# New instruction orders on four engines: an attention quad spread over two steps, beside the scans and in the last attention

## The reference

```
# state space layer, per sequence: 512 channels e, 16 states n
dA = exp(d_t[..., None] * A)
state = state * dA + (d_t * u_t)[..., None] * B_t[:, None, :]
y_t = einsum('ben,bn->be', state, C_t)
...
# causal attention, 16 heads of 32
scores = einsum('bqhd,bkhd->bhqk', q, k) * HEAD_DIM ** -0.5
attn = softmax(where(causal, scores, min))
ctx = einsum('bhqk,bkhd->bqhd', attn, v)
x = x + ctx @ wo
h = rms(x, w_ln2); logits = h @ w_router      # then 8 experts, top 2, and a shared one
```

## Time and profile before

| what | us |
|---|---|
| median of 3 runs | 1896.81 |
| lowest, highest | 1896.38, 1898.08 |
| the profiled run, its time | 1897.27 |
| the profiled run, its span | 1895.4 |
| VectorE busy | 1183.1 |
| TensorE busy | 1530.6 |
| scans of sequences 1, 2, 3: first to last start | 170 each (168 the third) |

### The profile page before, as it was taken

One profiled execution on the slowest core, in us unless ns is written; L12 is line 12 of the kernel. 1 busy time (PEld: TensorE's weight loads), 2 busy tenths in 40 slices (PEclk: granted clock), 3 DMA queues, 4 the chain that ended last, 5 costly groups with the idle time before them and its releaser, 6 DMA issues.

```text
span 1895.4 us, 26612 instructions
## 1 busy us (share of the span) xinstructions
PE 1530.6 (81%) x9104; PEld 1167.9 (62%) x9104; DVE 1183.1 (62%) x1731; ACT 888.1 (47%) x1974; POOL 810.3 (43%) x809
## 2 busy tenths in 40 slices
PE   5255877777967777957777799879999999999994
PEld 2134544555645555635556566668788899999973
DVE  4689658987568887489873444343332556565545
ACT  4443345664456664366652366212111566666510
POOL 0586135653145542266532321114431455555544
PEclk8555886888977888958887899989999999999997
DMA  5620000110100111001103200562220676777464
GB/s 192 244 75 26 23 6 25 60 51 28 46 17 34 51 46 31 27 23 51 45 29 117 89 29 29 195 233 83 99 85 1 223 270 234 269 236 267 151 232 160
DMA packets 94486, 195.74 MB, mean 103 GB/s; under 512 B 8769, under 2 KB 25665, under 8 KB 91025
## 3 DMA queue, kind: packets, MB, share of 16 engines
q1 hardware_dynamic: 89232, 177.26, 27.0%
q0 software_dynamic: 5120, 16.78, 2.6%
HBM read 140.40 MB, written 53.61 MB: 102 GB/s over the span
## 4 chain that ended last, share of the span: by engine, by line
PE 42%; issue 5%; DVE 5%; POOL 3%; ACT 2%; DMA 0%; DVEq 0%; ACTq 0%; SPq 0%; POOLq 0%
PE scores L588 20%; PE bank L588 12%; PE bank L770 2%; POOL yab L2162 2%; PE scores L707 2%; PE bank L720 1%; PE bank L652 1%; PE bank L735 1%; DVE YA L1552 1%; PE bank L960 1%; DVE HS L1542 1%; PE scores L710 1%; ACT PT L1180 1%; ACT bank L1137 1%; POOL lal L2155 1%
## 5 line engine op out<-in xcount | busy, mean ns | idle before, releaser
L1996 POOL TENSOR_TENSOR GB<-DU,BB 128x512 f32<-128x512 f32 x256 | 327.6, 1292 | 125.7 <-DVE HS L1542 67.6
L652 PE MATMUL bank<-ident,HS 128*128 128x128 f32 x896 | 184.9, 342 | 172.9 <-DVE YA L1552 118.0
L1542 DVE TENSOR_TENSOR_SCAN HS<-bank,GB 128x512 f32<-128x512 f32 x224 | 273.0, 1219 | 47.6 <-ACT bank L1137 23.9
L652 PEld LDWEIGHTS bank<-ident,HS 128*128 128x128 f32 x896 | 125.0, 172 | 222.3 <-DVE YA L1552 157.1
L1137 ACT ACTIVATE bank<-DL,aneg 128x512 f32<-128x512 f32 x224 | 154.9, 692 | 131.5 <-DVE HS L1542 130.2
L1552 DVE SCALAR_TENSOR_TENSOR YA<-bank,Ct,YA 128x512 f32<-128x512 f32 x224 | 164.3, 733 | 28.6 <-PE bank L652 26.5
L1180 ACT ACTIVATE PT<-bank 128x128 f32<-128x128 f32 (+3 forms) x256 | 110.5, 432 | 128.6 <-PE bank L720 125.9
L588 PE MATMUL scores<-xth,wgh 128*128 128x256 f32 x552 | 158.0, 286 | 2.0 <-DVE fa L1878 1.1
L588 PE MATMUL scores<-xth,wgl 128*128 128x256 f32 x552 | 156.1, 283 | 0.0
L588 PE MATMUL scores<-xtl,wgh 128*128 128x256 f32 x552 | 156.0, 283 | 0.0
L720 PE MATMUL bank<-ident,EX 128*128 128x128 f32 x640 | 129.8, 303 | 27.9 <-ACT PT L1180 25.8
(11 more groups left out here) (272 smaller groups left out, 3697.0 us busy)
## 6 DMA issues: line engine op xcount, KB each, us to landing
wgr<-wffn_in SPq DMA_DIRECT2D x108, 384.0 KB, 6.4
wdr<-wffn_in SPq DMA_DIRECT2D x81, 256.0 KB, 2.9
BB<-b_scratch SPq DMA_DIRECT2D x64, 256.0 KB, 3.2
xg<-V SPq DMA_DIRECT2D x1, 11776.0 KB, 40.2
xr<-xg SPq DMA_DIRECT2D x23, 512.0 KB, 5.7
yg<-ysb SPq DMA_DIRECT2D x23, 512.0 KB, 6.3
hah<-hhd SPq DMA_DIRECT2D x5, 1024.0 KB, 5.7
hal<-hhd SPq DMA_DIRECT2D x5, 1024.0 KB, 8.7
```

Source lines behind the costliest of these rows:

```text
L652: mm = nc.tensor.transpose(state_bank(s, q)[:, et * P:(et + 1) * P], HS[:, n % 2, et, tt * P:(tt + 1) * P], ident[:])
L1542: nc.vector.tensor_tensor_scan(HS[:, n % 2, et, :], decay_bank(s, k), GB[:, k % 4, :], 0.0, ALU.mult, ALU.add).then_inc(scan_done, 1)
L1996: nc.gpsimd.tensor_tensor(GB[:, k % 4, :], DU[:, et, :], BB[:, n % 2, :], ALU.mult).then_inc(gb_ready, 1)
```

## The change

The loop in `round_` is replaced on TensorE, ScalarE, VectorE and GpSimd by two functions on each, `units` (attention beside scans, three rounds) and `last_units` (attention 3). The round of scans alone keeps its order. The same instructions are issued with the same operands and waits, none is added or removed, and SyncE's order is as before. What differs is the order on each of the four engines. In `units`, k = 4q:

```diff
+            def units(b, s):
+                for q in range(-2, NQ + 1):
+                    now, next_, last = 0 <= q < NQ, 0 <= q + 1 < NQ, 0 < q
+                    i, m = quad(q)
+                    row = i - 1 if now and i else None
+                    if now:
+                        turn(b, HG * q + 1)
+                    if last:
+                        turn_states(s, T4 * (q - 1) + 1)
+                    if now:
+                        turn(b, HG * q + 2)
+                    if row is not None and m != 1:
+                        finish(b, row, (0, None, 1, 2)[m])
+                    if last:
+                        turn_states(s, T4 * (q - 1) + 2)
+                    if now:
+                        turn(b, HG * q + 3)
+                    if last:
+                        turn_states(s, T4 * (q - 1) + 3)
+                    if now:
+                        weigh(b, q)
+                    if next_:
+                        turn(b, HG * (q + 1))
+                    if now:
+                        turn_states(s, T4 * q)
+                    if q + 2 < NQ:
+                        scores(b, q + 2)
...
+            def last_units(b):
+                for q in range(-1, NQ):
+                    i, m = quad(q)
+                    if q + 1 < NQ:
+                        scores(b, q + 1)
+                    for a in range(HG):
+                        if q > 0:
+                            next(shared)
+                        if q >= 0 and a < HG - 1:
+                            turn(b, HG * q + a + 1)
+                        if q >= 0 and i and (m, a) in ((0, 1), (2, 1), (3, 2)):
+                            finish(b, i - 1, (0, 0, 1, 2)[m])
+                    if q + 1 < NQ:
+                        turn(b, HG * (q + 1))
+                    if q >= 0:
+                        weigh(b, q)
```

On ScalarE, `units`, and of `last_units` the part in which the tanh now stands ahead of the last `keep_turned`:

```diff
+            def units(b, s):
+                for q in range(-1, NQ + 1):
+                    now, next_ = 0 <= q < NQ, q + 1 < NQ
+                    i, m = quad(q)
+                    row = i - 1 if now and i else None
+                    v, w, k = HG * q, HG * (q + 1), T4 * q
+                    if now:
+                        keep_turned(b, v + 2)
+                    if next_:
+                        probs(b, w)
+                        probs(b, w + 1)
+                    if now:
+                        decay(s, k + 3)
+                        keep_turned(b, v + 3)
+                    if next_:
+                        probs(b, w + 2)
+                    if row is not None and m in (0, 2):
+                        finish(b, row, m + 1)
+                    if 0 < q + 1 < NQ:
+                        decay(s, k + 4)
+                    if next_:
+                        probs(b, w + 3)
+                    if now:
+                        keep_inverse(b, q)
+                    if next_:
+                        keep_turned(b, w)
+                        decay(s, k + 5)
+                    if row is not None and m == 1:
+                        finish(b, row, 2)
+                    if now:
+                        context(b, q)
+                    if next_:
+                        keep_turned(b, w + 1)
+                        decay(s, k + 6)
+                    if now and m == 3 and i + 1 < T4:
+                        finish(b, i, 0)
...
+                    if more:
+                        probs(b, w)
+                    keep_turned(b, v + 2)
+                    if more:
+                        probs(b, w + 1)
+                    for n in range(SE):
+                        if gate_end(n)[0] == q:
+                            early_tanh(n)
+                    keep_turned(b, v + 3)
+                    if more:
+                        probs(b, w + 2)
+                        probs(b, w + 3)
+                    if i and m == 2:
+                        finish(b, i - 1, 3)
+                    if m == 3 and more:
```

On VectorE, `units`; in `last_units`, `invert(q)` now stands at the start of quad q and the row's sum ahead of the shared expert's steps:

```diff
+            def units(b, s):
+                for q in range(-2, NQ + 1):
+                    now, next_, last = 0 <= q < NQ, 0 <= q + 1 < NQ, 0 < q
+                    i, m = quad(q)
+                    row = i - 1 if now and i else None
+                    k = T4 * q
+                    if row is not None and m == 3:
+                        finish(b, row, 3)
+                    if row is not None and m == 0:
+                        finish(b, row, 1)
+                    if last:
+                        add_state(s, k - 2)
+                    if row is not None and m == 2:
+                        finish(b, row, 2)
+                    if now:
+                        scan(s, k + 3)
+                    if last:
+                        add_state(s, k - 1)
+                    if next_:
+                        scan(s, k + 4)
+                    if now:
+                        context(b, q)
+                        add_state(s, k)
+                    if next_:
+                        invert(b, q + 1)
+                        scan(s, k + 5)
+                    if q + 2 < NQ:
+                        row_max(b, q + 2)
+                    if now:
+                        add_state(s, k + 1)
+                    if next_:
+                        scan(s, k + 6)
```

More of the change, by code:

```diff
@@ L869, in round_ @@
                     rotate(b, 7)
[L870 to L885 removed]
+                if att and scn:
+                    units(b, s)
+                elif scn:
+                    for q in range(NB):
+                        turn_states(s, q)
+                else:
+                    last_units(b)
                 if scn:
[L887 to L888 removed]
                     for tt in range(T4):
@@ L1337, in round_ @@
-                if att:
-                    keep_inverse(b, NQ - 1)
-                    context(b, NQ - 1)
-                if s == B:
-                    early_round(SE - 1)
+                if att and scn:
+                    units(b, s)
+                elif scn:
+                    for k in range(1, NB):
+                        decay(s, k)
+                        if k % 8 == 0 and k <= 8 * KC:
+                            round_weights(k // 8 - 1)
+                else:
+                    last_units(b)
@@ L1656, in early_ends, with last_units @@
                         early_up(n)
+            def units(b, s):
+                for q in range(-2, NQ + 1):
+                    now, next_, last = 0 <= q < NQ, 0 <= q + 1 < NQ, 0 < q
+                    i, m = quad(q)
+                    row = i - 1 if now and i else None
[26 more added lines that the diff above has]
+                        scan(s, k + 6)
+            def last_units(b):
+                row_max(b, 0)
+                for q in range(NQ):
+                    i, m = quad(q)
+                    more = q + 1 < NQ
+                    invert(b, q)
+                    if q:
+                        context(b, q - 1)
+                    if more:
+                        row_max(b, q + 1)
+                    if q == 0:
+                        low_down(0)
+                    if i and m == 0:
+                        finish(b, i - 1, 1)
+                    early_ends(q, False)
+                    if i and m > 1:
+                        finish(b, i - 1, m)
+                    early_ends(q, True)
+                context(b, NQ - 1)
             def round_(b, s):
```

214 lines of the change are left out of this document (78 added, 136 removed).

## The result

| | before | after |
|---|---|---|
| median, us | 1897.44 (1896.38 to 1898.5, 4 runs) | 1852.95 (1851.52 to 1853.62, 4 runs) |
| span of the profiled run | 1895.4 | 1851.2 |
| mean granted clock of TensorE | 0.861 | 0.878 |

The ratio of the times is 0.9761 [0.9747, 0.9775]: 44.5 us less, where 28.3 were forecast. The forecast of 1869.0 us was 16 us too slow.

The account below looks back on a forecast made before the run. VectorE's chain beside the scans was taken to bound the three rounds, TensorE attention 3. 1897.3 less 26.4 (three rounds of 13.9 - 5.1 = 8.8) less 1.9 gave 1869.0 us; forecast 1858 to 1882 (0.50), full range 1847 to 1894.

Parts of the forecast that it names:

- The stalls beside the scans: VectorE's waits for transposed states, scores, router product and first exponents beside the scans go: 13.9 us per round at full clock.
- What comes back at the lower clock: Row tiles 2 and 3, TensorE at 1.2 GHz 30% of the time: 5.1 us per round return, bounds 0 to 17.0.
- The floor doesn't move: VectorE's stall-free quad beside the scans stays at 9.28 us, since instructions and bank are the same; context only changes interval.
- rival 2: Waits move beside the scans: context late for its inverse, half a microsecond in 12 quads, 6 us a round; 1887 us, chance 0.18.
- The 1.6 us go: Start of a round: the first scan stands ahead of invert(0), so VectorE's 1.6 us wait for the first quad's exponents goes.
- Its scores are issued earlier: Beside the scans, scores two quads ahead come earlier while row_max comes behind the second next scan; 4.8 us of waits vanish.
- Rival 3: Slower: scores and a turn between two turn_states delay add_state beside the scans at the lower clock; 1909.6 us, chance 0.13.
- Net 1.9 us gained: Attention 3 as a whole: copies hidden in some quads, tanh in the way in others; bounds 8.1 gained and 3 lost.
- 6 x 0.5 = 3.0 us lost: Attention 3, six quads with a tanh: the last keep_turned queues behind it, making about 1.0 us where 0.54 stood.
- The 4.9 us saved: Attention 3, quads without tanh: the copy ahead of weigh is hidden, 9 x 0.54 us.
- Rival 1: Denser steps keep TensorE's upper clock, so all 41.7 us of stalls beside the scans go; 1847.5 us, chance 0.12.
- The signs: Expected in the changed profile: scan spans, the waits of nm, YA, invert and L731's instruction, and the first scan's start.

Follow-up runs that it names:

- experiment 7: Changed kernel with invert of the next quad ahead of the scan it now follows, as in the kernel before: 1855.97 us, ratio 0.9781.
- Experiments 2 to 4: Changed kernel with scores directly behind weigh again (1937.19 us), with row_max directly behind context again (1917.17 us), and with both (1903.87 us).
- experiment 2: Changed kernel with TensorE's scores of quad q + 2 directly behind weigh again: 1937.19 us, ratio 1.0204.
- experiment 8: Changed kernel with attention 3's tanh behind the last probs of the next quad, not ahead of the last keep_turned: 1843.08 us, ratio 0.9714.
- Experiment 9: Eight transposes that nothing reads, in six quads of each round: 1851.63 us added to the changed kernel, 1890.64 us added to the kernel before.
- experiments 4 and 6: Changed kernel with scores directly behind weigh and row_max directly behind context: 1903.87 us; changed kernel with only context moved back behind scan k + 5: 1884.16 us.

## Why the prediction was right, and where it fell short

**The stalls beside the scans: right, size included.** VectorE's waits for TensorE in the three rounds were 12.3, 13.1 and 11.2 us and are 2.8, 3.6 and 5.8: 24.4 us less. With the 1.0 us that each round's start gave (below) this is 27.4 us, where "8.8 us per round, three rounds 26.4" was forecast.

**What comes back at the lower clock: right in kind, too large.** It was put at 5.1 us per round, all of it in tiles 2 and 3. Of the waits for TensorE that are left only 1.8, 2.2 and 4.0 us lie there (from 355, 608 and 861 us on). The other 4.1 us of the three rounds lie in tiles 0 and 1, for which the sum had nothing. The share was taken from the kernel before, at a clock of 0.85, and the clock there is now 0.92, 0.92 and 0.89. At these the prediction's own 17.0 us give 2.7, 2.7 and 3.7 (an estimate), near to what came. That the mean of all waits left, 4.1 us per round, is near 5.1 is in part luck.

**"The floor doesn't move": wrong.** It rested on one interval of 3.11 us and three of 2.05, and said that `context` only changes its interval. A quad of tile 1 without stalls took 9.28 us and takes 9.08 (326.29 to 335.37, with one wait of 0.19 in it): `row_max`'s interval lost 0.22 us, and the one that `context` went to did not grow, since it had idle time too short for the list. That is 0.2 us a quad, 9.6 us in three rounds (an estimate from this one quad). The prediction gave the earlier `context` no price but the danger of rival 2.

**Waits for decays: not in the sum.** They were 8.6, 7.6 and 7.8 us and are 5.3, 6.0 and 5.0: 7.7 us less, which the stalls counted in the prediction had left out. It is not the short ones that went: of 0.16 to 0.25 us there were 52, 9.9 us in all, and are 48, 9.5 us. Of the longer ones there were 22, 14.0 us in all, and are 10, 6.8 us. Beside attention 0 half of these stood in the round's first quad and half in tile 3, as this one, and in tile 3 none is left:

```profile
419.34 1.22 DVE L1542 TENSOR_TENSOR_SCAN HS<-bank,GB 128x512 f32<-128x512 f32 x1 [0.48 <-ACT bank L1137]
```

I put that to ScalarE's new order, in which decays stand elsewhere among `probs` and copies. It is argued: no run undoes ScalarE's order alone.

**The end of a round: not in the sum.** The 6.7 us between the last scans and what comes next were not forecast, but for the 2.0 in it that are the starts of the second and third round. Behind the last scan beside attention 0 the last add ends 8.2 us after that scan's start, where it took 10.2; 1.4 us of this is `context`, which waits 0.32 us for its inverse and not 1.70. So the 42.4 us are: 24.4 of waits for TensorE and 7.7 for decays, less 2.2 of new waits for GB between the scans, 5.8 between first and last scans that no listed wait explains, and 6.7 behind the last scans. The 5.8 hold what `context` gave, and are less than the 9.6 estimated from one quad. They also hold that instructions follow each other more closely: beside attention 0 VectorE's busy time is 1.3 us less for the same 182 instructions (148.69, now 147.37), and a row begins some 0.08 us before the one ahead has ended. How they divide is not shown.

**"The 1.6 us go": in part.** The wait of `invert` went, but the first scan now waits 0.72 us for GB, since GpSimd's first product is only done 0.7 us after the end of `row_max`. Each round starts 1.0 us earlier after `row_max`, not 1.6 (rows at experiment 7).

**"Its scores are issued earlier": wrong in words.** On TensorE the scores stand later than before, behind a turn and a `turn_states`. `row_max` moved back by a scan and gave room for that. Experiments 2 to 4 show that the change needs both halves: without either, or without both, it loses to the kernel before. Rival 3 had seen the mechanism (scores between two `turn_states`), but as a danger of the new order, while in experiment 2 it is what the old place of the scores causes.

**Attention 3: the net was near, the terms were not.** "Net 1.9 us gained" stood against 3.6, less 1.9 in the expert stage. But "6 x 0.5 = 3.0 us lost" by the tanh is 8.4 us of attention 3 in experiment 8, 1.4 per tanh and not 0.5 (and 9.9 of the whole). It counted the tanh and the copy behind it. ScalarE's idle wait in front of the tanh, 0.75 to 2.92 us, and the two `probs` behind the copy, which TensorE's next turns want, were left out; those idle waits are 8.3 us in the six quads, about what the run gave back. The 4.9 us saved was too small in turn: without the tanh in the way the new order is worth 12.0 us there (130.6 against 118.6). The two terms were off by 5.4 and 7.1 us in opposite directions, so it is luck that the net was near.

**The rivals.** Rival 1 (the upper clock is kept, 1847.5 us) is half of what came: the clock rose to 0.92, and its size was nearer (5.5 us off, not 16), but its sum was all 41.7 us of stalls, and 12.2 of waits for TensorE stayed. Experiment 9 shows a clock raised by other means to be worth some 8 us in the old order. How much of the change's own gain is its higher clock no run separates. Rivals 2 and 3 had no sign in the trace: while the scans run, neither cn nor nm stands in the list of waits of any round (behind the last scan cn waits once, 0.3 us).

**The signs.** First to last scan start was put at 160 to 162 us and is 156 to 159. The wait of nm for scores is gone, as said. That of YA is under 3 us beside attentions 0 and 1 (2.1 and 2.2), and 4.5 beside attention 2. The waits of L731's instruction in attention 3 were to be about 6 us and are gone, but the turns wait 8.5. The first scan starts 0.72 us after the end of the first `row_max`, not within 0.3.

## What to carry to other kernels

Before calling the spacing of an engine's instructions a floor, look for the small idle times in it, those too short for a list of waits too: here an instruction of 0.27 us was free in an interval of 2.08 us and took 0.22 us off the one that it left. When engines hand work to each other, a new order is one change on all of them: test the parts apart, since each can be worse than none, and look at who else waits. In experiments 4 and 6 it was ScalarE, whose order those runs left alone. And count behind a late instruction in an in-order queue all that follows it until the next instruction of another engine that waits, and the wait in front of it too: here a 0.6 us tanh cost 1.4.

## What the hardware showed that was not expected

Transposes that nothing reads made the kernel before 0.36% faster (experiment 9), with the granted clock beside the scans at 0.86 and not 0.78, and TensorE busy for 122.84 us and not 128.84 though there was more for it to do. And it was not expected that a `context` of 0.27 us would fit at no cost between two scans that had stood 2.08 us apart without it: the add behind `context` starts 0.18 us after it (325.36, 325.54), the scan behind `invert` 0.09 us after that (326.20, 326.29), and the scans stand 2.07 us apart.
